# A four-stage transformer kernel on one core: five low halves and the last rows go to VectorE, a product moves across the end of a block, and the attention's order is planned with a later landing

## The reference

```
x = x + _layernorm(_L0_attn_ref(_layernorm(x), Wqkv, Wo))     # 32 heads of 16, one K and one V for all, causal, alibi
x = x + _layernorm(_L0_ffn_ref(_layernorm(x), gate, up, down))# (silu(x @ Wg) * (x @ Wu)) @ Wd, 512 -> 1376 -> 512, 4-bit weights
x = x + _layernorm(_L1_attn_ref(_layernorm(x), mask, w, b))   # one product with a block-masked 512 x 512 matrix
x = x + _layernorm(_L1_ffn_ref(_layernorm(x), W_base, ...))   # one product with a matrix made beforehand, 512 x 512
```

## Time and profile before

| what | us |
| --- | --- |
| median of 3 runs | 1140.46 |
| lowest and highest | 1137.76 and 1142.03 |
| the profiled execution | 1141.52 |
| its span, first to last instruction | 1139.8 |

### The profile page before, as it was taken

The page is one execution under the profiler, slowest core; times in us unless marked ns, Lnnn a source line. Parts: engine busy times, 40 slices in busy tenths (PEclk is TensorE's granted clock), DMA queues, the critical chain, the costliest instruction groups (busy, mean ns, idle before and its releaser), DMA issues. The chain is left out here.

```text
span 1139.8 us, 16312 instructions
## 1 busy us (share of the span) xinstructions
PE 1102.3 (97%) x5900; PEld 675.9 (59%) x5900; DVE 712.6 (63%) x1677; ACT 622.0 (55%) x1070; POOL 422.6 (37%) x494
## 2 busy tenths in 40 slices
PE   8889999999999999999999899999999999999997
PEld 7545354435334333334536676788788878777885
DVE  6787998996999999889622454440151151246674
ACT  5355766775787789977795344211211111126775
POOL 4463352343211543342165555321121111124765
PEclk9999999999999999999999999999999999999999
DMA  7434122203013121221220221330030032212111
GB/s 199 99 81 124 47 61 80 49 1 102 20 29 103 32 44 40 53 60 48 72 71 28 65 75 40 111 111 1 1 111 1 10 102 71 73 37 75 38 38 75
DMA packets 52813, 70.60 MB, mean 62 GB/s; under 512 B 14031, under 2 KB 31975, under 8 KB 51173
## 3 DMA queue, kind: packets, MB, share of 16 engines
q1 hardware_dynamic: 49004, 59.81, 18.7%
q0 software_dynamic: 3152, 8.63, 2.5%
q10 hardware_dynamic: 576, 1.11, 0.3%
HBM read 50.27 MB, written 18.87 MB: 61 GB/s over the span
## 5 line engine op out<-in xcount | busy, mean ns | idle before, releaser
L1143 ACT ACTIVATE PT<-ST,lowered 128x512 f32<-128x512 f32 x576 | 354.5, 694 | 64.2 <-PE PO L1538 33.4
L1234 DVE CUSTOM_DVE_ANT_0 bank<-bank,tail_mask 128x512 f32<-128x512 f32 x320 | 211.2, 721 | 24.9 <-PE bank L1440 24.4
L1440 PE MATMUL bank<-KS,QS 125*128 125x512 bf16 (+2 forms) x896 | 179.4, 305 | 8.9 <-DMA QS<-q_scratch 5.4
L1524 PE MATMUL ST<-QS,KS 128*128 128x512 bf16 x576 | 183.8, 382 | 3.9 <-ACT PT L1143 3.3
L1236 DVE TENSOR_REDUCE mx<-bank 128x2 f32<-128x512 f32 (+2 forms) x256 | 161.4, 680 | 25.9 <-PE bank L1440 14.4
L1538 PE MATMUL PO<-PT,V 128*32 128x512 f32 x1152 | 152.6, 604 | 0.6 <-POOL PT L1061 0.3
L1061 POOL TENSOR_SCALAR_AFFINE_SELECT PT<-PT 128x512 f32<-128x512 f32 x128 | 79.6, 649 | 176.1 <-ACT PT L1143 175.6
L1440 PEld LDWEIGHTS bank<-KS,QS 125*128 125x128 bf16 x896 | 73.5, 98 | 109.7 <-DVE mx L1234 31.7
L1792 POOL TENSOR_TENSOR f_h_part<-f_h,f_h_part 128x512 fp32r<-128x512 f32 (+1 forms) x44 | 56.7, 1288 | 217.2 <-ACT f_h_part L1835 217.1
L2006 PE MATMUL f_pair<-f_xT,gw 128*128 128x512 f32 (+1 forms) x344 | 136.6, 397 | 0.4 <-POOL gw L1781 0.3
L1902 DVE TENSOR_TENSOR f_h<-f_h,f_pair 128x512 f32<-128x512 f32 (+1 forms) x43 | 29.4, 685 | 170.7 <-ACT f_h L1828 170.7
(11 more groups left out here) (223 smaller groups left out, 1817.4 us busy)
## 6 DMA issues: line engine op xcount, KB each, us to landing
QS<-q_scratch SPq DMA_DIRECT2D x16, 384.0 KB
q_scratch<-QP SPq DMA_DIRECT2D x18, 256.0 KB, 2.2
QS<-q_scratch SPq DMA_DIRECT2D x16, 256.0 KB
xres<-_attn_hidden_states_dram POOLq DMA_DIRECT2D x16, 256.0 KB, 3.2
x_dram<-xout POOLq DMA_DIRECT2D x16, 256.0 KB, 2.4
xin<-x_dram SPq DMA_DIRECT2D x4, 1024.0 KB, 7.9
f_xsum<-x_dram SPq DMA_DIRECT2D x4, 1024.0 KB, 7.6
x_dram<-f_xsum SPq DMA_DIRECT2D x4, 1024.0 KB, 4.6
```

The costliest lines, as they stand in the source:

```text
L1143: act.activation(PT[:, quad % PT_RING, n % 4, :], ST[:, n % ST_RING, :], ACT.Exp, bias=lowered[:, 0:1]).then_inc(p_done, 1)
L1234: v.tensor_tensor_reduce(at(u), at(u), tail_mask[:, :], 1.0, -3e38, ALU.add, ALU.max, mx[:, i % 2, z, h:h + 1]).then_inc(bank_free_dve, 1)
L1440: last = pe.matmul(at(u)[:, j * w:(j + 1) * w], QS[0:ROWS1, slot, h + j, :], KS[b][0:ROWS1, k0:k0 + w], start=(j == 0 or not diag), stop=( ...
L1524: pe.matmul(ST[:, n % ST_RING, :], KS[b][0:ROWS2, kb * P:(kb + 1) * P], QS[0:ROWS2, slot, h:h + 4, :], start=True, stop=True).then_inc(st_ ...
```

## The change

There are four edits.

1. The planner is told that the first stack lands 6700 instead of 3500 ns after its start. This changes nothing else by itself, but the greedy planner makes another order of the whole attention from it.
2. For five tiles, the first of all and the last of each block (numbers 0, 10, 21, 32 and 43 of 44), the low half is made on DVE, behind `gated`, and no longer on POOL. `low_read` is the wait of the readers.
3. The `gate` product of tile 0 of blocks 2 and 3 moves in front of the last `down` of the block before ("first").
4. In the last stage the adding of step 14's two tiles moves from POOL to DVE.

```diff
-    end["stacked", 0] = 3500
+    end["stacked", 0] = 6700
...
+LOW_BY_DVE = [0] + [blk * NT + NT - 1 for blk in range(FB)]
...
-        events += [("gate", n), ("up", n)]
+        events += [("up", n)] if n == 0 and blk > 1 else [("gate", n), ("up", n)]
...
+    if 0 < blk < FB - 1:
+        events.append(("first", blk + 1))
     events.append(("down", NT - 1))
...
+        def low_read(eng, g):
+
+            if g in LOW_BY_DVE:
+                eng.wait_ge(h_lo_dve, LOW_BY_DVE.index(g) + 1)
+            else:
+                eng.wait_ge(h_lo, g + 1 - sum(x < g for x in LOW_BY_DVE))
+
+        def h_low(eng, blk, n):
+            w, s, g = tile_w(n), slot(blk, n), blk * NT + n
+            eng.wait_ge(h_hi, g + 1)
+            return eng.tensor_tensor(hi(h_parts[1][0:w, s, :]), h[0:w, s, :], h_parts[0][0:w, s, :], ALU.subtract)
...
-                    w, s = tile_w(n), slot(blk, n)
-                    pool.wait_ge(h_hi, blk * NT + n + 1)
-                    pool.tensor_tensor(hi(h_parts[1][0:w, s, :]), h[0:w, s, :], h_parts[0][0:w, s, :], ALU.subtract).then_inc(h_lo, 1)
+                    if blk * NT + n not in LOW_BY_DVE:
+                        h_low(pool, blk, n).then_inc(h_lo, 1)
...
                 v.tensor_tensor(h[0:w, s, :], h[0:w, s, :], banks(("gate", blk, n))[0:w, 1, :], ALU.mult).then_inc(h_ready, 1)
+                if g in LOW_BY_DVE:
+                    h_low(v, blk, n).then_inc(h_lo_dve, 1)
...
+                    elif kind == "first":
+                        project(n, 0, 0)
...
-                if k:
+                if 0 < k < STEPS - 1:
                     for t in range(2):
                         add(pool, k - 1, t)
...
                 sum_moments(v, STEPS - 1, range(t, t + 1))
+                add(v, STEPS - 2, t)
```

More of the change, by code:

```diff
@@ L1623, in pair_uses @@
         for kind, n in ffn_events(blk):
-            if kind in ("dq", "gate", "xt") + NEXT and (kind, blk, n) != FIRST_GATE:
-                use = (kind, blk + 1, n) if kind == "xt" else (kind, blk, n)
+            if kind in ("dq", "gate", "xt", "first") + NEXT and (kind, blk, n) != FIRST_GATE:
+                use = (kind, blk + 1, n) if kind == "xt" else ("gate", n, 0) if kind == "first" else (kind, blk, n)
                 slots.append((1 if kind == "gate" else 0) if blk == 0 else 1 - slots[-1])
@@ L1697, in ffn @@
         h_lo = sem("f_h_lo")
+        h_lo_dve = sem("f_h_lo_dve")
         y_tile = sem("f_y_tile")
@@ L1826, in silu @@
                 if g >= 2:
-                    act.wait_ge(h_lo, g - 1)
+                    low_read(act, g - 2)
                 act.activation(h[0:w, s, :], banks(("gate", blk, n))[0:w, 0, :], ACT.Silu).then_inc(sil_done, 1)
@@ L2013, in down @@
                 w, s, dw = tile_w(n), slot(blk, n), dq.dw[n // 2]
-                pe.wait_ge(h_lo, blk * NT + n + 1)
+                low_read(pe, blk * NT + n)
                 if blk == 0:
```

## The result

| kernel | median us | runs | lowest and highest |
| --- | --- | --- | --- |
| before | 1139.18 | 22 | 1137.46 and 1142.03 |
| changed | 1142.41 | 22 | 1140.20 and 1144.96 |

The ratio is 1.0028, with a 95% interval of 1.0021 to 1.0036: the changed kernel is 3.2 us slower, less than the 0.5% that the prediction called no change, but clear of noise. 1138.6 was forecast, 1.9 under the median of before as it was known then (1140.46, from three executions) and 0.6 under that of the 22. The time lies in the stated range and has moved the other way.

What follows compares the result with a forecast made beforehand. PE, busy 97% of the span, was taken as the bound. Terms summed to -1.9 on the 1139.8 us span; with 1.7 around it, and 1.06 off for the profiled run, 1138.6 was forecast, range 1133.6 to 1143.8.

Steps and rivals of the forecast that it cites:

- Low half of tile 0: Ahead of `down(0, 0)`: PE's wait and the low clock behind it go; -5.2 us, bounds -5.2 and -3.7.
- End of block 0: At the last low half of block 0: DVE makes it faster than POOL, shortening PE's wait; -0.6 us.
- Ends of blocks 1 and 2: Waits ahead of the last downs go, but new ones come at `down(2, 0)` and before `down(3, 0)`; net +1.5 us.
- Last rows: Last stage: DVE adds step 14's tiles while it would wait anyway, freeing POOL; -0.9 us, bounds -0.3 and -1.8.
- Start of the attention: First stack: PE's wait falls from 3.74 to 2.3 us, but the gain is waited away later; 0 us.
- a kept clock: Rival: the attention keeps the clock at its start, worth 1.6 to 4.2 us, giving 1135.9; chance 0.24.
- End of the attention: Uncovered wait before `wo` of block 15, later cuts behind `fin` of block 13; +1.8 us, bounds +0.5 and +3.
- Rest of the attention: Another order of the same work, priced by the density of PE's waits; +1.5 us, bounds -2 and +4.
- The base: Whole kernel: span 1139.8 us plus 1.7 around it, the profiled run (1141.52) taken as 1.06 above its median.
- The rival on the slow side: The clock falls in four new or longer waits at block ends and attention's end; 5.8 us, 1144.4; chance 0.12.
- the join: At `down(0, 0)`: behind PE's wait 12 products ran at a clock of 0.64, costing 1.45 us more.
- The fourth rival: The attention's new order is dearer: +4 at its bound and +3 at the tail, 1142 us; chance 0.14.

Runs made afterwards that it cites:

- join_only: The kernel before with only the low half of tile 0 of the first block moved to DVE: 1134.52 us, ratio 0.9957.
- low_and_rows: The changed kernel with the old attention order (3500) and no gate product moved, keeping the five low halves and last rows on DVE: 1132.30 us, ratio 0.9939.
- start_moved: low_rows_apart with the first 16 steps of PE and 13 of DVE taken from the new order: 1128.88 us, ratio 0.9904.
- order_only: The kernel before with only the planner's value set to 6700, the three other edits taken back: 1147.37 us, ratio 1.0066.
- rest_without_order: The changed kernel with the planner's value set back to 3500, all other edits kept: 1134.80 us, ratio 0.9958.
- low_rows_apart: low_and_rows with DVE's additions of the last stage set where POOL isn't making the last scales: 1130.94 us, ratio 0.9928.
- before_again: The kernel before, unchanged, run once more: 1140.80 us, ratio 1.0008.
- order_7200: low_rows_apart with the attention order planned with the value 7200: 1136.76 us, ratio 0.9975.

## Why the prediction was wrong, by its own steps

- **Low half of tile 0 (-5.2).** Right, in its place, size and cause; join_only has 4.9 to 5.6. POOL's pieces stayed hidden but for the 0.3 us that PE waited for one of them before as well.
- **End of block 0 (-0.6).** Right: a wait of 0.20 is left.
- **Ends of blocks 1 and 2 (+1.5).** Right: +1.6 in the table, and 2.2 to 2.5 where low_and_rows gives 2.7. An edit reads the wrong way when the moved work was also somebody's cover; counting from S, the start of the last down, found it.
- **Last rows (-0.9, bounds -0.3 and -1.8).** Right in sign, wrong in size: 0.2. The step that failed is the choice of the additions' cover as free. DVE was idle, but POOL was not.
- **Start of the attention (0).** Near for the changed kernel: the wait came out as forecast (2.0 against 2.3), 1.8 us of waiting came back in front of the first turn, and at an equal clock 0.7 us are won up to 120 us. Alone, with the old order behind it, the start gains 2.1 (start_moved), of which 1.2 are shorter waits and the rest clock. Whether the clock stays up more often with this start is open: between 29 and 34 us it was below 1.00 in five of six traces with the old start and no filling and in two of six with the new one, but four of those with the new start and the new order behind it had 0.83 or 0.91 between 40 and 60 us. The prediction gave a kept clock a quarter of the chances.
- **End of the attention (+1.8).** Right: 1.4 to 1.9, with 1.46 in front of the output product of block 15 where 1.6 was forecast. No wait of `pv` for the cuts shows; the rest is in small waits.
- **Rest of the attention (+1.5, bounds -2 and +4).** This is the step that failed. With order_only at +7.5, less the start's -2.1 and the end's +1.9, the middle costs some 7.7 us, beyond its upper bound. The traces give 5.5 (against rest_without_order) to 6.5 (against low_and_rows, at an equal clock), and 3.4 of it lies at 440 to 480 us in both. The rest of the 7.7 is about what the start gains alone (2.1) and doesn't gain in front of the new order (0.7). Why the stretch at 440 us is dear, beyond DVE's fullness, stays open. I had priced a re-plan by the density of waits in the old order. But the old order is the outlier of its 18, 5.1 us ahead of the next by the planner's own count, and the best of the new 18 is planned 7.1 us later. Waits must be expected to be denser in a new draw than in a kept best one; that this is the reason is argued here, from two draws (6700 and 7200), and not shown.
- **The base.** The sum was hung on one execution, taken as 1.06 us over the median. Over 22 runs that execution is 2.3 us over it; it lost its clock at two places at the start, which is the likely reason, and the profiled execution of the changed kernel is 1.6 us under its own. A term on the clock in a trace is a term with a chance, not a fact of the kernel.

The rival on the slow side (1144.4, four new waits at the 1.45 us of the join) had the right sign for a wrong reason: around the three waits of 1.3 to 1.6 us that did come, at 622 to 628, 837 to 842 and 931 to 936 us, the granted clock of the changed kernel's trace is 1.00. Nor does a wait of 1.61 us bring it down each time: the same wait ahead of the third turn left it at 1.00 between 80 and 90 us in rest_without_order, join_only, low_and_rows and low_rows_apart, where before and before_again have 0.66. The fourth rival, the dearer order at 1142, had 0.14 and is what happened in kind. That its time fits so well is luck: it had +4 for the middle, where 5.5 to 7.7 were lost, and +3 for the end, where 1.4 to 1.9 were.

With the measured terms the sum is -5.2 - 0.6 + 1.5 - 0.2 - 2.1 + 1.9 + 7.7 = +3.0 on 1139.2, against 3.2 measured. The last three are order_only's 7.5 by construction, so what this shows is only that the order and the other edits add up.

## What to carry to other kernels

An edit to one number that a search reads is a re-plan of everything behind it: price it as a new draw, and compare the ends that the search itself plans before anything is run, and take over the part that is wanted by hand (the start here, 2.1 us) while the rest stays as it was. Work that is moved in front of the point on which another engine's chain hangs is taken from that chain's cover: count both sides from that point. And before a small operation is moved to an idle engine, look at what the engine that shares its memory path does at that moment.

## What the runs showed of the hardware

- POOL's operations on a single column take 0.52 and 1.01 us beside DVE additions with both inputs in SBUF, 0.19 and 0.56 alone. Four normalizations on DVE took 3.83 us beside two POOL subtractions (2.92), and 1.93 and 2.50 apart from each other.
- The granted clock of TensorE behind the same wait of 3.4 to 3.9 us for the first stack was 0.66 (before, before_again), 0.72, 0.51 and 0.50 between 29 and 34 us in five traces and 1.00 in a sixth, that of low_and_rows. With the wait filled by unused products it was 1.00 in both traces with 15 of them, and the executions of a kernel filled at three places lie within 0.6 us.
- At one mean granted clock the executions of a kernel still differ by up to 3 us (0.994 in before_again: 1137.78 to 1140.80).
- A kernel with more waits can have as high a mean clock and be slower: order_7200 lies at 0.997 to 0.999 and takes 1136.8 us, low_rows_apart at 0.996 to 0.998 and takes 1130.9.
